# Cross-attention with a mixture of experts: late expert weights fetched into the projection weights' space, pad rows copied from an image in DRAM

## The reference, cut to what matters

```python
q1, k1, v1 = heads(xn @ Wq1), heads(xn @ Wk1), heads(xn @ Wv1)
q2, k2, v2 = heads(ctx @ Wq2), heads(ctx @ Wk2), heads(ctx @ Wv2)
out1 = softmax(q2 @ k1.T * 64 ** -0.5) @ v1
out2 = softmax(q1 @ k2.T * 64 ** -0.5) @ v2
a = sigmoid(alpha_attn)
x = x + merge(out1 * a + out2 * (1 - a)) @ Wout + bout
...
w, idx = top_k(softmax(layernorm(x) @ gate_w.T), 4)
w = w / sum(w)
x = x + sum_k(w[k] * ((silu(h @ w1[idx[k]]) * (h @ w3[idx[k]])) @ w2[idx[k]]))   # h = layernorm(x)
```

## Time and profile before

| | us |
|---|---|
| median of 3 runs (2154.18 to 2159.37) | 2157.95 |
| the profiled execution | 2155.32 |
| its span in the profile | 2153.5 |
| TensorE busy | 1907.1 (89%) |
| VectorE busy | 1417.3 (66%) |
| ScalarE busy | 1261.0 (59%) |
| GpSimd busy | 1211.3 (56%) |

### The profile page before, as it was taken

How to read it: one execution, slowest core, us unless ns; L and a number is a source line. 1 busy time by engine, 2 the same in 40 slices (tenths; PEclk the granted TensorE clock), 3 DMA queues, 4 the chain that set the end, 5 groups by cost and what they waited for, 6 DMA issues and landing times.

```text
span 2153.5 us, 53309 instructions
## 1 busy us (share of the span) xinstructions
PE 1907.1 (89%) x15778; PEld 1642.3 (76%) x15779; DVE 1417.3 (66%) x3205; ACT 1261.0 (59%) x3605; POOL 1211.3 (56%) x1683
## 2 busy tenths in 40 slices
PE   5999999999999999999999999999369999999100
PEld 4788888888888878888888888878269999999100
DVE  4567666667666666766666766666536666666577
ACT  4766666676666666666666666667136556555100
POOL 2466666566666566666566666556426666666200
PEclk9999999999999999999999999999679999999655
DMA  5610111101111110111101111110766666666798
GB/s 149 153 36 35 42 49 47 34 34 34 39 49 49 34 34 34 39 45 48 39 34 34 38 45 49 39 34 26 189 158 184 180 182 179 184 184 179 276 371 317
DMA packets 158596, 210.54 MB, mean 98 GB/s; under 512 B 24273, under 2 KB 131425, under 8 KB 158562
## 3 DMA queue, kind: packets, MB, share of 16 engines
q1 hardware_dynamic: 119394, 127.75, 20.7%
q0 software_dynamic: 26112, 71.86, 9.2%
q10 hardware_dynamic: 13056, 10.50, 1.7%
HBM read 113.02 MB, written 97.03 MB: 98 GB/s over the span
## 4 chain that ended last, share of the span: by engine, by line
PE 82%; DMA 7%; issue 3%; DVE 3%; SPq 3%; POOL 2%; ACT 1%; DVEq 0%; POOLq 0%; ACTq 0%
PE p_s L1047 12%; PE p_av L1145 12%; PE p_pt L1129 12%; PE p_s L1111 10%; PE p_gu L1300 9%; PE p_x L1180 5%; PE p_y L1318 4%; PE p_s L1057 4%; DMA z<-mid_rows 3%; PE p_xt L1289 3%; DMA out_dram<-z 2%; PE p_x L1047 2%; PE p_pt L1047 2%; PE p_av L1057 2%; PE p_pt L1057 2%
## 5 line engine op out<-in xcount | busy, mean ns | idle before, releaser
L512 POOL TENSOR_TENSOR probs<-probs,inv 128x256 f32<-128x256 f32 x1024 | 596.0, 614 | 434.0 <-DVE inv L844 433.3
L603 ACT ACTIVATE probs<-p_s,nmx 128x256 f32<-128x256 f32 x1024 | 475.3, 488 | 67.5 <-DVE nmx L837 62.7
L837 DVE TENSOR_REDUCE nmx<-p_s 128x4 f32<-128x1024 f32 x256 | 313.1, 1223 | 140.3 <-PE p_s L1111 136.7
L544 POOL DMA_INDIRECT y_rows<-y_out,xg x288 | 276.3, 959 | 177.8 <-issue 107.9
L504 POOL DMA_INDIRECT x_rows<-routed,slot_i x256 | 252.5, 986 | 170.0 <-DVE target L829 95.8
L1129 PEld LDWEIGHTS p_pt<-ident,probs 128*128 128x128 f32 x2048 | 222.2, 141 | 87.5 <-issue 62.4
L1129 PE MATMUL p_pt<-ident,probs 128*128 128x128 f32 x2048 | 280.0, 280 | 7.5 <-issue 4.9
L1145 PE MATMUL p_av<-probsT,val 128*64 128x256 f32 x2048 | 280.0, 394 | 6.5 <-DVE probsT L741 5.8
L741 DVE COPY probsT<-p_pt 128x512 f32<-128x512 f32 x256 | 176.1, 688 | 109.8 <-PE p_pt L1129 107.1
L1047 PE MATMUL p_s<-rowsT_hi,wp_hi 128*128 128x256 f32 x768 | 231.6, 302 | 8.3 <-DVE wp_lo L857 8.3
L591 ACT COPY probsT<-p_pt 128x512 f32<-128x512 f32 x256 | 152.5, 596 | 137.4 <-PE p_pt L1129 117.3
(11 more groups left out here) (183 smaller groups left out, 4712.5 us busy)
## 6 DMA issues: line engine op xcount, KB each, us to landing
xg<-x_rows SPq DMA_DIRECT2D x144, 257.0 KB
y_in<-y_rows SPq DMA_DIRECT2D x32, 1024.0 KB, 6.7
rows<-in_ctx_dram SPq DMA_DIRECT2D x32, 256.0 KB, 2.7
x_in<-in_x_dram SPq DMA_DIRECT2D x32, 256.0 KB, 2.7
mid_rows<-x_mid SPq DMA_DIRECT2D x32, 256.0 KB, 2.2
z<-mid_rows SPq DMA_DIRECT2D x32, 256.0 KB, 7.4
out_dram<-z ACTq DMA_DIRECT2D x32, 256.0 KB, 5.7
y_rows<-y_out,xg POOLq DMA_INDIRECT x288
```

What stands on the lines that cost most here:

```text
L512: pool.tensor_tensor(pr[:, h, t, :], pr[:, h, t, :], rc[:, g:g + 1].to_broadcast([P, S]), ALU.mult).then_inc(normed_p, 1)
L544: pool.indirect_dma_start(y_rows, bass.IndirectOffsetOnAxis(ap=xg[r][:, i, D:D + 1].bitcast(I32), axis=0), y_out[r % 4][:, i, :], None).th ...
L603: act.activation(probs[u % 2][:, h, t, :], p_s[:, 2 * (u % 2) + h, t * S:(t + 1) * S], ACT.Exp, bias=nmx[u % 2][:, g:g + 1], accum_out=sum ...
L837: dve.tensor_reduce(nmx[i][:, :], p_s[:, 2 * i:2 * i + 2, :].rearrange("p h (t k) -> p (h t) k", t=ST), AX.X, ALU.max, negate=True).then_i ...
```

## The change

1. `wp` is now the first tensor of the first phase, so that `late_slots` (the first of the second phase, 48 KB per partition as `wp`) lies on `wp` alone; the low parts of the expert weights lie on queries, keys, values and transposed rows. SP fetches the late pieces when the last projection of the last sample is done (`proj_done`), and VectorE makes five of the twelve low parts ahead of its wait for the last output projection, the other seven behind the plan.
2. A new DRAM tensor `pad_image` holds the pads of all 16 experts as whole rows. It is filled once, behind the fill of the fixed region and by the same function, `fill_pads`; the target column is written as four equal numbers (16 bytes) to the row's end. `pad_experts` copies an expert's 256 rows from the image with one DMA. The two fills are four DMAs (64 counts of the semaphore), and SP and ScalarE wait for them before the copies.
3. On SP the table is read back after its first two experts' copies, not after all eight.

```diff
+    pad_image = nc.dram_tensor("pad_image", [E * GROUP, ROW], F32, kind="Internal").ap()
...
+            wp = [sb("wp_hi", [P, 6, KT, INNER], F32R, a), sb("wp_lo", [P, 6, KT, INNER], F32R, a)]
             qT = ...
             kT = ...
-            wp = [sb("wp_hi", [P, 6, KT, INNER], F32R, a), sb("wp_lo", [P, 6, KT, INNER], F32R, a)]
+            val = [sb(f"val{d}", [P, ST, INNER], stack=a) for d in range(2)]
+            rowsT = ...
             gate_rows = sb("gate_rows", [E, D], stack=a)
...
-            pad_target = sb("pad_target", [P, 2 * E, 2], I32, a)
+            pad_target = sb("pad_target", [P, 2 * E, 2, ROW - D], I32, a)
...
-        def pad(eng, row, n, groups):
-            to = x_rows[bass.ds(row, groups * GROUP), :].rearrange("(n p) d -> p n d", p=P)
-            eng.dma_start(to[:, :, 0:D], spread(bias[:, :], 1, [P, 2 * groups, D])).then_inc(pads_sent, 16)
-            eng.dma_start(to[:, :, D:D + 1].bitcast(I32), flat(pad_target[:, n:n + groups, :]).unsqueeze(2),
+        def fill_pads(eng, rows_to, n):
+            to = rows_to.rearrange("(n p) d -> p n d", p=P)
+            eng.dma_start(to[:, :, 0:D], spread(bias[:, :], 1, [P, 2 * E, D])).then_inc(pads_sent, 16)
+            eng.dma_start(to[:, :, D:ROW].bitcast(I32), pad_target[:, n:n + E, :, :].rearrange("p e n c -> p (e n) c"),
                           allow_slow_non_contiguous=True).then_inc(pads_sent, 16)
+        FILLED = 64
         def pad_experts(eng, experts):
             for e in experts:
                 row = eng.value_load(base_i[0:1, e:e + 1], min_val=e * REGION, max_val=e * REGION + TOKENS)
-                pad(eng, row, e, 1)
+                eng.dma_start(x_rows[bass.ds(row, GROUP), :],
+                              pad_image[e * GROUP:(e + 1) * GROUP, :]).then_inc(pads_sent, 16)
...
-            pad(sp, E * REGION, E, E)
+            fill_pads(sp, x_rows[E * REGION:, :], E)
+            fill_pads(sp, pad_image[:, :], 0)
...
-            sp.wait_ge(outp_done, B)
+            sp.wait_ge(proj_done, PROJS * B)
             for n in range(LATE):
                 load_piece(late, n, late_in)
...
-            pad_experts(sp, range(0, E, 2))
+            sp.wait_ge(pads_sent, FILLED)
+            pad_experts(sp, range(0, 4, 2))
             sp.wait_ge(table_out, 16)
             sp.dma_start(table_row[:, :, :], group_table.rearrange("(a v) n -> a v n", a=1)).then_inc(table_in, 16)
+            pad_experts(sp, range(4, E, 2))
             sp.wait_ge(rows_sent, 16 * ST * TOP_K * B)
-            sp.wait_ge(pads_sent, 32 * (E + 1))
+            sp.wait_ge(pads_sent, FILLED + 16 * E)
...
             act.wait_ge(plan_step, 15)
+            act.wait_ge(pads_sent, FILLED)
             pad_experts(act, range(1, E, 2))
...
+            LATE_AHEAD = 5
+            def late_pieces(first, end):
+                for n in range(first, end):
+                    dve.wait_ge(late_in[n], arrived(late, LATE_SLOTS, n))
+                    slot, _, hi, lo = late[n]
+                    dve.tensor_tensor(lo, slot, hi.bitcast(F32), ALU.subtract).then_inc(late_lo, 1)
...
+                if prev and not cur:
+                    late_pieces(0, LATE_AHEAD)
                 if prev:
                     dve.wait_ge(outp_done, pb + 1)
...
-            for n in range(LATE):
-                dve.wait_ge(late_in[n], arrived(late, LATE_SLOTS, n))
-                slot, _, hi, lo = late[n]
-                dve.tensor_tensor(lo, slot, hi.bitcast(F32), ALU.subtract).then_inc(late_lo, 1)
+            late_pieces(LATE_AHEAD, LATE)
```

More of the change, by code:

```diff
@@ L119, in xattn_moe_kernel @@
         with ExitStack() as a:
+            wp = [sb("wp_hi", [P, 6, KT, INNER], F32R, a), sb("wp_lo", [P, 6, KT, INNER], F32R, a)]
             qT = [[sb(f"qT{d}_{part}", [P, PAIRS, S], F32R, a) for part in ("hi", "lo")] for d in range(2)]
             kT = [[sb(f"kT{d}_{part}", [P, PAIRS, S], F32R, a) for part in ("hi", "lo")] for d in range(2)]
-            wp = [sb("wp_hi", [P, 6, KT, INNER], F32R, a), sb("wp_lo", [P, 6, KT, INNER], F32R, a)]
+            val = [sb(f"val{d}", [P, ST, INNER], stack=a) for d in range(2)]
+            rowsT = [[sb(f"rowsT{i}_{part}", [P, KT, S], F32R, a) for part in ("hi", "lo")] for i in range(2)]
             gate_rows = sb("gate_rows", [E, D], stack=a)
-            val = [sb(f"val{d}", [P, ST, INNER], stack=a) for d in range(2)]
             rows = sb("rows", [P, ST, D], stack=a)
-            rowsT = [[sb(f"rowsT{i}_{part}", [P, KT, S], F32R, a) for part in ("hi", "lo")] for i in range(2)]
             x_in = sb("x_in", [P, ST, D], stack=a)
@@ L482, in _ @@
                                base=0, pattern=[[1, P]], channel_multiplier=-1).then_inc(consts_set, 1)
-            pool.iota(pad_target[:, :, :], [[GROUP, 2 * E], [P, 2]], base=DUMP, channel_multiplier=1).then_inc(consts_set, 1)
+            pool.iota(pad_target[:, :, :, :], [[GROUP, 2 * E], [P, 2], [0, ROW - D]], base=DUMP, channel_multiplier=1).then_inc(consts_set, 1)
             pool.memset(mhalf[:, :], -0.5).then_inc(consts_set, 1)
```

## The result

| | before | changed |
|---|---|---|
| median of 4 runs, us | 2158.23 | 2172.41 |
| lowest to highest | 2154.18 to 2159.37 | 2169.86 to 2175.83 |
| the profiled execution / its span | 2155.32 / 2153.5 | 2169.86 / 2168.1 |

The ratio is 1.0068, 95% interval 1.0051 to 1.0086: 14.2 us slower, where 8.6 had been forecast.

What follows compares the result with a forecast made beforehand. TensorE carries 82% of the chain of waits, so only its two gaps matter: fills +19.8 us, hand-over -11.2 us (late-weights' +2.0 included), together +8.6, giving 2166.5 us against the median; range 2152 to 2177.

Steps and rivals of the forecast that it cites:

- the main step: Before the x load on SP: the second fill delays TensorE one for one, +19.8 us, bounds +5.6 to +26.4.
- The fills on SP: Two fills instead of one ahead of the next sample's loads: x lands 2f - 19.8 us later, f one fill's cost; +19.8.
- the slack ahead of x: First gap, 100 to 110 us: VectorE already waits 5.12 us for x, TensorE 4.01, so added SP work delays TensorE fully.
- the fill's price: Cost f of one fill in SP's queue: 19.8 us, with 16-byte pieces priced like 4-byte ones; bounds 12.7 to 23.1.
- The rival of cheap fills: First gap: 16-byte pieces move like full rows, f 12.7, stall grows only 5.6 us; total 2148.6 to 2152.4; chance 0.10.
- The late weights and the early low parts: End of attention: moving the weights costs nothing; five early parts slow three scatters, plan ends 2.0 us later (1.2 to 3.0).
- The pads: Hand-over: copies replace pad pairs, last pad lands at 1564.5 instead of 1575.7, -11.2 us with the +2.0 included (-15 to -5).
- about 0.5 for table issues and wait: Hand-over, SP's queue: the table's issues, wait for its landing and reload add about 0.5 us between second and third copies.
- The price of a copied row: Hand-over: 55 ns per DRAM-to-DRAM row, between half of 77.4 ns and all of it; 14 us for all copies.
- the prediction's own sign: Hand-over check: if copies land 25 us or more after the table leaves, the step on their price is wrong.
- The rival of dear copies: Hand-over: a copied row costs 77.4 ns, gaining only 5 us; +19.8 - 5 = +14.8, total 2173 us; chance 0.18.

## Why the prediction came out as it did

The direction, the range and the main step were right, the size was not: +14.2 against +8.6.

1. **The fills on SP.** Forecast +19.8 us, measured +16.5, inside its bounds. That the slack ahead of x was below zero and would be passed on one for one is what the traces and the added fill alone (+17.3) show. What was too large is the fill's price: if both fills cost the same, the added one delays x by f, so f is 16.5 and not 19.8. The rival of cheap fills, with +5.6 for the stall, falls: pieces of 16 bytes cost what those of 4 cost (landing after 21.4 and 22.1 us, against 22.6 before in the earlier trace rows). By the Trainium skill, "DMA: Bandwidth & Descriptors", section "Specifications", both are read-modify-writes below 512 bytes; the trace agrees in that they cost the same.
2. **The late weights and the early low parts.** The late weights left at 1510.29, which is the 1493.8 of the forecast and 16.5, and no early low part waited for them, as forecast. The early low parts were to cost +2.0 us by the scatter row of before; measured +1.5, with three slow scatters as counted. The Trainium skill, "SBUF — State Buffer", section "Who interferes with whom", infers that such a tensor_tensor leaves descriptor generation alone. The scatters of 1.97, 8.53 and 14.21 us say that it does hold up a scatter. A scatter also takes its row numbers, `slot_i`, from SBUF, and the traces do not tell which of the two parts is held.
3. **The pads.** This step failed. Forecast: last copy landed 18.7 us behind the plan. Measured: 1587.57 - 1561.83 = 25.7. The term that was wrong is "about 0.5 for table issues and wait". With it the table was to be read back 5.1 us after its issue (1.4, two copies of 1.6, and 0.5); it was 10.4. The row of before showed 15.3 us for the table's landing, and I had put that down to the queue it shared. The table has its own 10.4 us, and while its writes are under way the copies stand too, so their data had to move behind it: from there to the last landing it was 15.4 us, against the forecast's 13.6 (six copies of 1.6, and 4 to land). That is 5.3 and 1.7 us of the 7.0. The price of a copied row, 55 ns, was about right: at 237 to 350 GB/s it is 48 to 70 ns. By the prediction's own sign, copies landing 25 us or more after the table leaves, this price would have been at fault: the sign came true and pointed at the wrong term. With the table spread the last copy landed 19.0 us behind the table's issue, near the 18.7.
4. **The rest**, +2.9 us, lies in later phases, and its cause is open.

Sum by traces: +16.5 + 1.5 - 6.3 + 2.9 = +14.6 us of span. The rival of dear copies gave nearly this total (+14.8) for another reason, and it would have been wrong to take the total as its proof. Against the forecast, the hand-over gained 6.3 us where 13.2 had been forecast (31.9 less 18.7), 6.9 less; the fills cost 3.3 less, the low parts 0.5 less, and later phases added 2.9. 6.9 - 3.3 - 0.5 + 2.9 = 6.0 us, and 14.6 - 8.6 is 6.0: the whole miss in the spans. That it is no larger is in part luck: the fills were priced 3.3 us too high and the gain at the hand-over 6.9 us too high, and these two errors partly cancel.

## What to carry to other kernels

Before adding a transfer, look for the first load behind it in the same queue and for who waits on that: where the slack is already negative the transfer costs its full time, and behind the load it costs nothing (17 us against 0 for the same 4 MB). When a small store is late, test it alone before blaming the queue: here 2 KB written in pieces of 4 bytes side by side took 10.4 us where a copy of 260 KB took 3.2, and it held up the rest. What a change gains at one end has to be read with what it brings at the other: as it stood this one lost 14 us, and with its fills behind the loads and its table turned it is 24 us faster than the kernel before, of which the kernel before could have had 8 by moving its own fill.

## What the runs showed of the hardware that was not expected

- 512 writes of 4 bytes into 2 KB of DRAM: 10.4 to 12.2 us in seven runs, some 20 ns each, while in the changed kernel the other transfers of the core all but stood still (2 to 10 GB/s). The same writes 512 bytes apart: 1.8 us, in one run.
- A copy DRAM to DRAM of 256 rows of 1040 bytes goes as packets of 16.6 KB, one per DMA engine, and takes 3.2 us by itself. Cut to 1028 of 1040 bytes it goes row by row, and the hand-over takes 8 us more.
- A GpSimd scatter beside a loop of VectorE subtractions with two SBUF inputs took 1.97 us in most runs, and 8.53 or 14.21 us, the whole loop, in two. What decides between them was not tried.
- The kernel before took 2158 and 2162 us on two chips and 2470 and 2506 on two others. In the traces from the slower ones ScalarE is idle for 8 us, 28 times. The cause was not found.
